# Attention units of 250 queries instead of 375, full PSUM banks, and two steps between changes of TensorE's tiling

## The chip, the cores and the metric

One core of a Trainium2 chip runs the whole program in one launch. The metric is the device time of that launch in microseconds (us). TensorE (PE in the profile) does the matrix products, VectorE (DVE) and ScalarE (ACT) read its results out of PSUM, GpSimd (POOL) works in SBUF and issues indirect DMAs, SyncE's queue (SPq) issues the direct ones.

## The reference

An audio tower of two layers over 8 streams (B = 8) of 750 tokens and 64 features: a convolutional tokenizer, then attention, a mixture of 8 experts, a phase-memory block and a second mixture, each with a residual. Only the attention of layer 0 is touched:

```python
q = jnp.einsum('btd,hrd->bhtr', x, Q)      # x: layer-normed h, (8, 750, 64); Q: (8, 32, 64)
k = jnp.einsum('bud,hrd->bhur', x, K)
scores = jnp.einsum('bhtr,bhur->bhtu', q, k) / sqrt(d)
attn = jax.nn.softmax(scores, axis=-1)
ctx = jnp.einsum('bhtu,bud->bhtd', attn, x)
out = jnp.einsum('bhtd,hde->bte', ctx, VO)  # VO: (8, 64, 64)
```

All of it is float32: 8 streams, 8 heads of 32 features, 750 queries against 750 keys.

## The kernel before, in words

**Units and steps.** The attention stage works in units of one stream, one pair of heads (`hp`, 4 of them) and one part of the queries (`th`). Before, a part is half of the queries (`HALF` = 375), so there are 8 x 4 x 2 = 64 units (`NQ`), and a unit has 6 steps, one for each tile of 125 keys (`c`): 384 steps. `place(m)` gives a unit's stream, pair and part.

**A step on TensorE** (the loop at the end of the stage, `for m ... for c ...`):

- `scores_t` (L627), one matmul for each of the two heads: transposed scores, 125 keys x 375 queries, with 32 contraction rows, into a PSUM bank of its own.
- the jobs of `maxima(m, c)`, two `score` jobs (L576): scores of the unit two ahead, untransposed, 125 queries x 375 keys, of which only the row maximum is wanted. They go to the ring (below). The unit two ahead is of the other pair of heads, so they lie on the two 32-row groups of the array that `scores_t` doesn't use.
- `shifts` (L638), bf16, 3 contraction rows: subtracts each query's maximum from the transposed scores by accumulation in the same bank.
- `values(x - 1)` (L654) of the step before: exp(scores) of 125 keys x 375 queries against the tokens, two heads as two column tiles of 64, accumulated over the six steps in the one bank `ctx_bank`.
- the other ring jobs due at this step (`ring_jobs`).

**The ring.** Three PSUM banks (0 to 2) are used in turn by all jobs that are not part of the step itself. Job k of the order list `order` takes bank k % 3, and TensorE waits on `ring_free` until job k - 3 has been read out. The jobs: `score` (read by VectorE's `reduce_max`, L1578), `shift` (a transposition of the maxima, L582), `proj` (queries and keys, L565, read by ScalarE, L1291), `out` (context times VO and the row sums, L616, read by VectorE: L1627, L1628, and after every second one L1632, L1633), `xt`, `logits` and `pos` (layer norm transposes and routing of the mixture, L590, L601, L608). Every engine walks through the same list in the same order, so VectorE reads the ring in the order in which TensorE fills it.

**From maxima to shift.** When the last `score` job of a unit has been reduced, VectorE joins the maxima (L1582), POOL splits them into three bf16 parts (five instructions, L1067 to L1071), TensorE transposes them (`shift`), VectorE copies them (L1588), and SyncE's queue writes them with two DMAs into `NS_` (L938), from where `shifts` reads them.

**Other banks.** Two pairs of banks (3 to 6, `st_bank`) hold the transposed scores of alternating steps; ScalarE's `exp_` reads one pair at a time (L1300) into one of four SBUF buffers. `ctx_out` (ScalarE, L1308) copies `ctx_bank` to SBUF after a unit's last step; `values` of the next unit waits for it.

**Around the stage.** Ahead of the loop, `before` holds 4 projections, and the maxima and shifts of units 0 and 1. Behind it, `after` holds the outputs and the routing of the last stream. `side_jobs` puts layer norms and routing of other engines at fixed steps.

The waits that matter:

```python
pe.wait_ge(ring_free[k % 3], k // 3)        # ring: wait for the job three before
pe.wait_ge(S["exp_done"], x - 1)            # scores_t of step x
pe.wait_ge(S["ctx_out"], m)                 # values, first step of unit m
```

Of the kernel before, what the change touches and what calls it, by code (L numbers as in the profile page):

```python
# [15 lines left out]
BF16 = mybir.dt.bfloat16  # L16
# [3 lines left out]
AX = mybir.AxisListType.X  # L20
# [4 lines left out]
HALF = L // 2  # L25
NB, KT = 9, 3
# [23 lines left out]
def build(nc, t, out):  # L50
    with ExitStack() as ctx:
# [89 lines left out]
        QH, at = view(0, [2, 2, L])  # L141
        KH, at = view(at, [2, 2, L])
        NS_, at = view(at, [2, HALF + 1], BF16)
        CT, at = view(at, [2, 4, L])
        PR, at = view(at, [4, 2, HALF], parts=R)
        MX, at = view(at, [2, 2, 6], parts=R)
        M1, at = view(at, [2, 6], parts=R)
        MR, at = view(at, [2, 6], parts=R)
        NM, at = view(at, [2, 18], BF16, parts=R)
        MT, at = view(at, [2, 126], BF16, parts=18)  # L150
# [154 lines left out]
        NU = 4 * B  # L305
# [49 lines left out]
        NQ = 8 * B  # L355

        def place(m):

            b, u = divmod(m, 8)
            return b, u // 2, u % 2  # L360

        def maxima(m, c):

            return [("score", m + 2, 2 * c + h2) for h2 in range(2)] if m + 2 < NQ else []

        def ring_jobs(m, c):

            b, hp, th = place(m)
            s = 12 * hp + 6 * th + c
            found = []  # L370
            if c == 1 and 2 <= m + 1 < NQ:
                found.append(("shift", m + 1))
            if b == 0 and s in (2, 3, 4, 5):
                found.append(("proj", 0, 1, (s - 2) // 2, s % 2))
            if b + 1 < B and s in (14, 16, 18, 20):
                found.append(("proj", b + 1, 0, (s - 14) // 4, (s - 14) // 2 % 2))
            if b + 1 < B and s in (26, 28, 30, 32):
                found.append(("proj", b + 1, 1, (s - 26) // 4, (s - 26) // 2 % 2))
            if b > 0 and 3 <= s < 27 and s % 2 == 1:
                found.append(("out", b - 1, (s - 3) // 4, (s - 3) // 2 % 2))  # L380
            if b < 2 and s in (24, 27):
                found.append(("xt", 1, b + 2, (s - 24) // 3))
            if b > 0:
                found += {35: [("xt", 2, b - 1, 0)], 36: [("xt", 2, b - 1, 1)], 38: [("logits", b - 1)],
                          42: [("pos", b - 1)]}.get(s, [])
            return found

        def side_jobs(m, c):

            b, hp, th = place(m)  # L390
            s = 12 * hp + 6 * th + c
            found = []
            if b < 2 and s in (4, 8, 15, 19):
                found.append(("ln_mean" if s in (4, 15) else "ln_std", 1, b + 2 + NP * (s >= 15)))
            if b > 0:
                if s in (28, 32):
                    found.append(("ln_mean" if s == 28 else "ln_std", 2, b - 1))
                if s == 39:
                    found += [("choose", b - 1), ("weigh", b - 1)]
                if s == 44:  # L400
                    found.append(("slots", b - 1))
                if s >= 45:
                    found += [("scatter", b - 1, 2 * (s - 45)), ("scatter", b - 1, 2 * (s - 45) + 1)]
# [9 lines left out]
        order = before + [x for m in range(NQ) for c in range(6)  # L413
                          for x in maxima(m, c) + ring_jobs(m, c) + side_jobs(m, c)] + after
# [63 lines left out]
        def _(pe):  # L478
# [74 lines left out]
            def ring(job):  # L553
# [5 lines left out]
                if kind == "proj":  # L559
                    _, b, g, qk, th = job  # L560
                    p, a = b % NP, b // NP
                    if ("xt", 1, b, 1) in ring_at:
                        ring_emptied(pe, ("xt", 1, b, 0))
                        ring_emptied(pe, ("xt", 1, b, 1))
                    last = pe.matmul(ps[:, 0:HALF], qkp[:, a, qk, g * 128:(g + 1) * 128],  # L565
                                     XT[:, p * L + th * HALF:p * L + (th + 1) * HALF], start=True, stop=True)
                elif kind == "score":
                    _, q, i = job
                    b, hp, th = place(q)
                    h2, half, j = i % 2, i // 2 % 2, 3 * th + i // 4  # L570
                    g, row = hp // 2, 64 * (hp % 2) + 32 * h2
                    if i == 0 and q % 4 == 0:
                        for qk in range(2):
                            for part in range(2):
                                ring_emptied(pe, ("proj", b, g, qk, part))
                    last = pe.matmul(ps[0:R, 0:HALF], QH[row:row + 32, b % 2, g, j * R:(j + 1) * R],  # L576
                                     KH[row:row + 32, b % 2, g, half * HALF:(half + 1) * HALF],
                                     start=True, stop=True, tile_position=(row, 0))
                elif kind == "shift":
                    q = job[1]  # L580
                    pe.wait_ge(S["shift_in"], q + 1)
                    last = pe.transpose(ps[0:18, 0:63].bitcast(BF16)[:, 0:R],  # L582
# [27 lines left out]
                else:  # L610
                    _, b, j, h = job
# [1309 lines left out]
```

## Time and profile before

| what | value |
|---|---|
| median of 3 runs | 1637.41 us (1635.68 to 1638.0) |
| the profiled execution | 1635.87 us |
| its span, first to last instruction | 1634.0 us |
| mean granted TensorE clock over the span | 0.854 of full |
| TensorE busy | 1303.5 us (80%) |
| VectorE busy | 986.9 us (60%) |
| ScalarE busy | 588.3 us (36%) |
| GpSimd busy | 443.3 us (27%) |

### The profile page before, as it was taken

Reading aid. Unit: us, or ns where it says so; the run is one execution under the profiler, and the core shown is the slowest. Engines: PE = TensorE matmul, PEld = TensorE weight load, DVE = VectorE, ACT = ScalarE, POOL = GpSimd, SP = SyncE. Lnnn points to the kernel's source line nnn. Section 1 sums busy time; section 2 is a strip of 40 time slices with the busy share of each in tenths; the row PEclk is TensorE's granted clock in tenths of the full one; section 3 lists DMA queues with packets and bytes.
Section 4 is the critical chain, followed back from the end, with each engine's and each line's share of the span. In section 5 each row is a group of like instructions: output and inputs, shape, how many; then the busy total and the mean of one; then the engine's idle time right before and its main releaser. Section 6 shows DMA issues by size and latency. Waiting matters only on the chain.

```text
span 1634.0 us, 21800 instructions
## 1 busy us (share of the span) xinstructions
PE 1303.5 (80%) x8045; PEld 668.8 (41%) x8045; DVE 986.9 (60%) x2165; ACT 588.3 (36%) x933; POOL 443.3 (27%) x797
## 2 busy tenths in 40 slices
PE   5589999999999999999999961750437658565895
PEld 4343344444444444444444331320216456454664
DVE  3355576666666666656667430212688988742798
ACT  1314444434444444444443310220144244322552
POOL 3112022302314013031130132007862362642000
PEclk9769999999999999999999855785667758656898
DMA  2100000000000000000000011121200000000000
GB/s 70 21 1 2 1 2 2 6 1 2 3 1 2 1 2 2 1 1 2 2 2 2 1 27 29 22 52 16 19 3 1 1 1 1 11 1 1 5 18 17
DMA packets 45974, 14.36 MB, mean 9 GB/s; under 512 B 43194, under 2 KB 44314, under 8 KB 45869
## 3 DMA queue, kind: packets, MB, share of 16 engines
q1 hardware_dynamic: 41261, 11.06, 3.1%
q0 software_dynamic: 4608, 1.91, 1.3%
q8 instruction: 65, 1.06, 0.3%
q14 instruction: 40, 0.33, 0.1%
HBM read 6.67 MB, written 7.17 MB: 8 GB/s over the span
## 4 chain that ended last, share of the span: by engine, by line
PE 64%; DVE 21%; POOL 5%; issue 4%; SPq 3%; DMA 2%; ACT 1%; POOLq 0%; DVEq 0%; ACTq 0%
PE psum L627 19%; PE psum L654 19%; PE psum L576 4%; PE psum L616 3%; PE psum L565 3%; PE psum L638 3%; DVE arena L1888 2%; DVE arena L1887 2%; PE psum L698 2%; DVE arena L1882 1%; SPq L952 1%; POOL lnst L1038 1%; SPq L926 1%; PE psum L710 1%; DVE lnst L1549 1%
## 5 line engine op out<-in xcount | busy, mean ns | idle before, releaser
L1578 DVE TENSOR_REDUCE arena<-psum 125x1 f32<-125x375 f32 x768 | 385.2, 543 | 227.3 <-PE psum L576 221.5
L1300 ACT ACTIVATE arena<-psum 125x750 f32<-125x750 f32 x384 | 305.9, 797 | 462.6 <-PE psum L638 456.8
L576 PE MATMUL psum<-arena 32*125 32x375 f32 x1536 | 385.2, 535 | 0.8 <-ACT arena L1291 0.7
L627 PE MATMUL psum<-arena 32*125 32x375 f32 x1536 | 352.7, 536 | 0.0
L654 PE MATMUL psum<-arena,XN 125*64 125x375 f32 x1536 | 333.9, 514 | 0.0
L627 PEld LDWEIGHTS psum<-arena 32*125 32x125 f32 x1536 | 115.6, 184 | 153.4 <-issue 130.7
L654 PEld LDWEIGHTS psum<-arena,XN 125*64 125x64 f32 x1536 | 77.1, 136 | 174.5 <-issue 173.8
L576 PEld LDWEIGHTS psum<-arena 32*125 32x125 f32 x1536 | 136.1, 184 | 23.7 <-DVE arena L1578 21.0
L638 PE MATMUL psum<-arena,onesb 3*125 3x375 bf16 x768 | 128.2, 327 | 0.0
L1067 POOL TENSOR_SCALAR arena<-arena 125x6 bf16<-125x6 f32 x64 | 15.9, 249 | 377.8 <-DVE arena L1582 377.4
L1142 POOL DMA_INDIRECT XN<-expert_out,slot_out x48 | 63.5, 1324 | 107.7 <-DMA expert_out<-arena 93.8
L540 PE MATMUL psum<-ident,XN 125*128 125x125 f32 x84 | 18.0, 379 | 91.9 <-POOL XN L1039 73.8
L784 PE MATMUL psum<-ident,arena 125*128 125x125 f32 x48 | 16.8, 361 | 70.2 <-DVE arena L1776 69.9
L616 PE MATMUL psum<-vox,arena 128*125 128x130 f32 x384 | 69.1, 307 | 3.8 <-DVE arena L1628 3.8
L1467 ACT ACTIVATE arena<-psum,wall 128x375 f32<-128x375 f32 x96 | 55.0, 574 | 45.2 <-PE psum L875 38.6
L638 PEld LDWEIGHTS psum<-arena,onesb 3*125 3x125 bf16 x768 | 54.0, 134 | 37.1 <-issue 3.1
L616 PEld LDWEIGHTS psum<-vox,arena 128*125 128x125 f32 x384 | 51.5, 195 | 40.5 <-issue 33.9
L1122 POOL DMA_INDIRECT expert_in<-XN,slot_in x48 | 58.8, 1226 | 23.2 <-issue 15.0
L565 PE MATMUL psum<-XT,qkp 128*128 128x375 f32 x128 | 59.2, 550 | 0.7 <-ACT XT L1277 0.7
L1038 POOL TENSOR_TENSOR lnst<-lnst,mhalf 125x12 f32<-125x12 f32 x14 | 32.2, 2298 | 99.8 <-DVE lnst L1558 99.8
L1269 ACT ACTIVATE arena<-XN 125x768 f32<-125x768 f32 x14 | 11.7, 839 | 124.4 <-DVE XN L1551 124.4
L1627 DVE RECIPROCAL arena<-psum 125x4 f32<-125x4 f32 x96 | 17.4, 182 | 59.2 <-PE psum L616 59.2
(322 smaller groups left out, 1989.6 us busy)
## 6 DMA issues: line engine op xcount, KB each, us to landing
arena<-arena SPq DMA_DIRECT2D x128, 2.2 KB
expert_in<-XN SPq DMA_DIRECT2D x8, 250.0 KB
arena<-expert_in SPq DMA_DIRECT2D x8, 250.0 KB
expert_out<-arena SPq DMA_DIRECT2D x8, 250.0 KB
out<-H SPq DMA_DIRECT2D x8, 187.5 KB
expert_in<-XN,slot_in POOLq DMA_INDIRECT x48
XN<-expert_out,slot_out POOLq DMA_INDIRECT x48, 3.9
arena<-in_L_ffn_w SPq DMA_DIRECT2D x2, 256.0 KB, 4.3
```

The source lines that it names most:

```text
L565: last = pe.matmul(ps[:, 0:HALF], qkp[:, a, qk, g * 128:(g + 1) * 128], XT[:, p * L + th * HALF:p * L + (th + 1) * HALF], start=True, stop ...
L576: last = pe.matmul(ps[0:R, 0:HALF], QH[row:row + 32, b % 2, g, j * R:(j + 1) * R], KH[row:row + 32, b % 2, g, half * HALF:(half + 1) * HAL ...
L616: last = pe.matmul(ps[0:R, i * 130:(i + 1) * 130], CT[:, b % 2, hp, j * R:(j + 1) * R], vox[:, hp, :], start=True, stop=True)
L627: pe.matmul(st_bank[x % 2][h2][0:R, 0:HALF], KH[row:row + 32, b % 2, g, c * R:(c + 1) * R], QH[row:row + 32, b % 2, g, th * HALF:(th + 1) ...
L638: last = pe.matmul(st_bank[x % 2][h2][0:R, 0:HALF], onesb[row:row + 3, 0:R], NS_[row:row + 3, th, 0:HALF], start=False, stop=True, tile_po ...
L654: last = pe.matmul(ctx_bank[64 * h2:64 * h2 + 64, 0:HALF], XN[:, p, c, a, :], PR[:, x % 4, h2, :], start=(c == 0), stop=(c == 5), tile_pos ...
L1038: link(pool.tensor_tensor(lnst[:, 3, p, :], lnst[:, 2, p, :], mhalf[0:R, 0:2 * NJ], ALU.pow))
L1122: pool.indirect_dma_start(out=xbuf, out_offset=bass.IndirectOffsetOnAxis(ap=slot_in[:, g:g + 1], axis=0), in_=XN[:, p, j, a, :], in_offset ...
L1142: pool.indirect_dma_start(out=XN[:, p, j, a, :], out_offset=None, in_=ybuf, in_offset=bass.IndirectOffsetOnAxis(ap=slot_out[:, g:g + 1], a ...
L1300: act.activation(PR[:, x % 4], psum[0:R, 3 + 2 * (x % 2):5 + 2 * (x % 2), 0:HALF], ACT.Exp)\
L1467: act.activation(dst, ps[:, 0:HALF], ACT.Relu, bias=b_).then_inc(done, 1)
L1578: dve.reduce_max(MX[:, q % 2, i // 2 % 2, col:col + 1], ps[0:R, 0:HALF], AX).then_inc(done, 1)
```

## The change

- A unit is one stream, one pair of heads and one third of the queries (`THIRD` = 250): 96 units, 3 steps each, 288 steps. A step takes two key tiles, so that a bank holds 2 x 250 = 500 columns.
- In a step the `shifts` come first (one matmul of 500 columns for each head, `start=True`), then `scores_t` of the first key tile, then `score` jobs, then `scores_t` of the second key tile, and then a second pair of `score` jobs where there is one.
- A unit has 6 `score` jobs of 500 columns instead of 12 of 375: a query tile against keys 0 to 499 (two tiles, two heads), and both query tiles against keys 500 to 749 in one bank. `max_step` sets their steps; two jobs fall on a step, but four on each of the first six steps, and the last nine have none.
- TensorE takes the steps in pairs: everything of steps k and k + 1 up to the scores, then `values(k - 2)`, the ring jobs due at k, `values(k - 1)`, and the ring jobs due at k + 1. ScalarE's order: `exp_(k)`, a `ctx_out` if one is due, `exp_(k + 1)`, a `ctx_out` if one is due, then projections.
- Projections are split by half of the streams (`a`): 64 contraction rows each, two jobs in a row on the two 64-row groups of the array. Queries and keys of all 8 streams are kept, so all projections are made in the first three streams. The outputs are split likewise: `out_pair` issues both jobs of a query tile together, 8 matmuls of 65 columns, alternating between two row groups and two ring banks.
- `before` holds 8 projections (4 pairs), and the maxima and shift of unit 0 only.

```diff
-        NQ = 8 * B
+        NQ = 12 * B
...
+        def max_step(k):
+
+            return (k - 3) // 2 if k < 15 else k - 9
+
+        max_at = {}
+        for k in range(3, 3 * NQ):
+            max_at.setdefault(max_step(k), []).append((k // 3, k % 3))
+        shift_at = {min(max_step(3 * q + 2) + 2, 3 * q - 1 - q % 2): q for q in range(1, NQ)}
+
+        def maxima(x):
+
+            return [("score", q, 2 * tile + h2) for q, tile in max_at.get(x, []) for h2 in range(2)]
...
+        proj_at = {(0, 1 + i): job for i, job in enumerate(projections(0, 1))}
+        for p in range(1, NP):
+            for i, job in enumerate(projections(p, 0) + projections(p, 1)):
+                proj_at[(p - 1, 6 + 2 * i)] = job
+
+        def ring_jobs(x):
+
+            b, s = divmod(x, 36)
             found = []
+            if x in shift_at:
+                found.append(("shift", shift_at[x]))
+            if (b, s) in proj_at:
+                found += [proj_at[(b, s)] + (a,) for a in range(2)]
+            if b > 0 and 3 <= s < 15 and s % 2 == 1:
+                found += [("out", b - 1, (s - 3) // 2, h) for h in range(2)]
+            if b < 2 and s in (31, 33):
+                found.append(("xt", 1, b + 2, (s - 31) // 2))
             if b > 0:
+                found += {21: [("xt", 2, b - 1, 0)], 22: [("xt", 2, b - 1, 1)], 24: [("logits", b - 1)],
+                          27: [("pos", b - 1)]}.get(s, [])
             return found
...
-        before = [("proj", 0, 0, qk, th) for qk in range(2) for th in range(2)]
-        for q in range(2):
-            before += [("score", q, i) for i in range(12)] + [("shift", q)]
+        before = [job + (a,) for job in projections(0, 0) for a in range(2)]
+        before += [("score", 0, i) for i in range(6)] + [("shift", 0)]
...
+        order = before + [job for x in range(0, 3 * NQ, 2) for job in
+                          maxima(x) + maxima(x + 1) + ring_jobs(x) + side_jobs(x) + ring_jobs(x + 1) + side_jobs(x + 1)] + after
...
+            def out_pair(b, j):
+
+                for h in range(2):
+                    k = ring_at[("out", b, j, h)]
+                    if k >= 3:
+                        pe.wait_ge(ring_free[k % 3], k // 3)
+                if j == 0:
+                    pe.wait_ge(S["ctx_out"], 12 * (b + 1))
+                for hp in range(4):
+                    for h in range(2):
+                        r = slice(64 * h, 64 * h + 64)
+                        ps = ring_bank[ring_at[("out", b, j, h)] % 3]
+                        last = pe.matmul(ps[0:R, hp * (D + 1):(hp + 1) * (D + 1)], CT[r, b % 2, hp, j * R:(j + 1) * R],
+                                         vox[r, hp, h * (D + 1):(h + 1) * (D + 1)], start=True, stop=True,
+                                         tile_position=(64 * h, 0))
+                        if hp == 3:
+                            last.then_inc(S["ring_full"], 1)
...
+                if h2 == 0:
+                    if x >= 2:
+                        pe.wait_ge(S["exp_done"], x - 1)
+                    if cc == 0:
+                        pe.wait_ge((S["shift_dma0"], S["shift_dma1"])[m % 2], 32 * (m // 2 + 1))
+                pe.matmul(st_bank[x % 2][h2][0:R, 0:2 * THIRD].rearrange("r (i c) -> r i c", i=2), onesb[row:row + 3, 0:R],
+                          NS_[row:row + 3, th, :].unsqueeze(1).to_broadcast([3, 2, THIRD]),
                           start=True, stop=False, tile_position=(row, 0))
...
+            ring_in(before)
+            for k in range(0, 3 * NQ, 2):
+                for x in (k, k + 1):
+                    mx = maxima(x)
                     for h2 in range(2):
+                        shifts(x, h2)
                     for h2 in range(2):
+                        scores_t(x, 0, h2)
+                    ring_in(mx[0:2])
+                    for h2 in range(2):
+                        scores_t(x, 1, h2)
+                    ring_in(mx[2:])
+                if k:
+                    values(k - 2)
+                    ring_in(ring_jobs(k))
+                    values(k - 1)
+                ring_in(ring_jobs(k + 1) if k else ring_jobs(k) + ring_jobs(k + 1))
+            values(3 * NQ - 2)
+            values(3 * NQ - 1)
...
-            for m in range(NQ):
-                for c in range(6):
-                    exp_(m, c)
-                    if c == 0 and m:
-                        ctx_out(m - 1)
...
+            for x in range(0, 3 * NQ, 2):
+                exp_(x)
+                if x >= 2 and (x - 2) % 3 == 2:
+                    ctx_out((x - 2) // 3)
+                exp_(x + 1)
+                if x >= 2 and (x - 1) % 3 == 2:
+                    ctx_out((x - 1) // 3)
...
+                    h2, tile = i % 2, i // 2
+                    if tile < 2:
+                        dve.reduce_max(MX[:, q % 2, 0, 2 * h2 + tile:2 * h2 + tile + 1], ps[0:R, 0:2 * THIRD], AX)\
+                           .then_inc(done, 1)
+                    else:
+                        dve.reduce_max(MX[:, q % 2, 1, 2 * h2:2 * h2 + 2],
+                                       ps[0:R, 0:2 * THIRD].rearrange("r (n c) -> r n c", n=2), AX).then_inc(done, 1)
```

The rest of the diff fits sizes (`MX`, `M1`, `NM`, `MT`, `NS_`, `QH`, `KH`, `PR`), counts of semaphores and the steps of the side jobs to the new units. The three ring banks, the two pairs of score banks, the four buffers of `exp_` and the one `ctx_bank` stay.

## Rows read from the trace of the kernel before

**Rows 1.** Stretches: busy us (instructions) of PE, PEld, DVE, ACT, POOL; clock; DMA.

```profile
104.00:110.80 6.80, 6.80 (x35) 3.01 (x34) 2.31 (x5) 1.59 (x2) 0.00 (x0) 0.50 0.01 3
110.80:926.60 815.80, 815.66 (x5888) 333.86 (x5882) 527.28 (x1222) 357.14 (x501) 182.45 (x516) 1.00 0.01 2
926.60:958.50 31.90, 31.90 (x99) 10.43 (x98) 2.07 (x11) 7.79 (x11) 12.62 (x24) 0.50 0.02 1
```

**Rows 2.** Timeline of TensorE, one step with a shift ahead and a projection behind.

```profile
809.88 0.22 PE L582 MATMUL psum<-identb,arena 125*18 125x125 bf16 x1
810.03 0.58 PE L627 MATMUL psum<-arena 32*125 32x375 f32 x2
810.04 0.66 PE L576 MATMUL psum<-arena 32*125 32x375 f32 x2
810.45 0.48 PE L627 MATMUL psum<-arena 32*125 32x375 f32 x2
...
810.76 0.33 PE L638 MATMUL psum<-arena,onesb 3*125 3x375 bf16 x2
811.02 0.85 PE L654 MATMUL psum<-arena,XN 125*64 125x375 f32 x4
811.80 0.90 PE L565 MATMUL psum<-XT,qkp 128*128 128x375 f32 x2
812.63 0.58 PE L627 MATMUL psum<-arena 32*125 32x375 f32 x2
```

**Rows 3.** Timeline of all engines, step 1 right behind step 0, half clock.

```profile
105.41 0.82 PE L576 MATMUL psum<-arena 32*125 32x375 f32 x1
...
105.67 1.00 DVE L1578 TENSOR_REDUCE arena<-psum 125x1 f32<-125x375 f32 x2 [1.36 <-PE psum L576]
105.71 0.83 PE L627 MATMUL psum<-arena 32*125 32x375 f32 x2
...
106.27 0.28 PEld L576 LDWEIGHTS psum<-arena 32*125 32x125 f32 x1 [0.23 <-DVE arena L1578]
```

**Rows 4.** Groups of instructions by form in the stage: VectorE's maximum.

```profile
L1578 DVE TENSOR_REDUCE arena<-psum 125x1 f32<-125x375 f32 x744 | 372.8, 543 | 206.2 <-PE psum L576 200.4 <-issue 3.8
```

**Rows 5.** Timeline of all engines where a unit ends: its last values, then ScalarE's copy.

```profile
406.86 0.85 PE L654 MATMUL psum<-arena,XN 125*64 125x375 f32 x4
...
407.75 0.48 ACT L1308 ACTIVATE arena<-psum 128x375 f32<-128x375 f32 x1
```

**Rows 6.** Timeline of TensorE around one output job.

```profile
210.60 0.71 PE L616 MATMUL psum<-vox,arena 128*125 128x130 f32 x4
211.24 0.58 PE L627 MATMUL psum<-arena 32*125 32x375 f32 x2
```

**Rows 7.** Timeline of VectorE behind a second output job.

```profile
215.74 0.17 DVE L1627 RECIPROCAL arena<-psum 125x4 f32<-125x4 f32 x1
215.94 0.42 DVE L1628 TENSOR_TENSOR arena<-psum,arena 125x256 f32<-125x256 f32 x1
...
217.49 0.23 DVE L1633 TENSOR_TENSOR H<-H,arena 125x64 f32<-125x64 f32 x1
```

**Rows 8.** Chain of waits ahead of the loop (start, us, what).

```profile
74.67 5.35 PE psum L565 x8
...
80.54 0.14 issue
...
91.69 9.55 PE psum L576 x24
...
101.26 0.56 DVE arena L1578
...
104.06 0.92 PE psum L627 x2
```

**Rows 9.** Timeline of TensorE, one step of the last twelve, at half clock.

```profile
929.81 1.61 PE L627 MATMUL psum<-arena 32*125 32x375 f32 x4
...
933.11 1.61 PE L627 MATMUL psum<-arena 32*125 32x375 f32 x4
```

More of the change, by code:

```diff
@@ L353, in build @@
         ln_at = {x: k for k, x in enumerate(lns)}
-        NQ = 8 * B
+        NQ = 12 * B
         def place(m):
[L359 to L369, printed above, removed]
-            found = []
[L371 to L382, printed above, removed]
+            b, u = divmod(m, 12)
+            return b, u // 3, u % 3
@@ L569, in ring @@
                     b, hp, th = place(q)
-                    h2, half, j = i % 2, i // 2 % 2, 3 * th + i // 4
+                    h2, tile = i % 2, i // 2
                     g, row = hp // 2, 64 * (hp % 2) + 32 * h2
-                    if i == 0 and q % 4 == 0:
+                    if i == 0 and q % 6 == 0:
                         for qk in range(2):
                             for part in range(2):
[L575 to L578, printed above, removed]
+                                ring_emptied(pe, ("proj", b % NP, g, qk, part, b // NP))
+                    parts = [(tile, 0, 2 * THIRD, 0)] if tile < 2 else [(n, 2 * THIRD, L, n * THIRD) for n in range(2)]
+                    for n, lo, hi, at_ in parts:
+                        j = 2 * th + n
+                        last = pe.matmul(ps[0:R, at_:at_ + hi - lo], QH[row:row + 32, b, g, j * R:(j + 1) * R],
+                                         KH[row:row + 32, b, g, lo:hi], start=True, stop=True, tile_position=(row, 0))
                 elif kind == "shift":
@@ L609, in ring @@
                     last = pe.matmul(ps[0:R, 0:NJ * E0], ones[0:R, 0:R], SO[:, 0:NJ, :], start=False, stop=True)
-                else:
-                    _, b, j, h = job
-                    for i in range(2):
-                        hp = 2 * h + i
-                        if j == 0 and i == 0:
-                            pe.wait_ge(S["ctx_out"], 8 * b + 4 * h + 4)
-                        last = pe.matmul(ps[0:R, i * 130:(i + 1) * 130], CT[:, b % 2, hp, j * R:(j + 1) * R],
-                                         vox[:, hp, :], start=True, stop=True)
@@ L665, in _, with ring_in @@
+                last.then_inc(S["pv_done"], 1)
+            def ring_in(jobs_):
+                for job in jobs_:
+                    if job[0] == "out":
+                        if job[3] == 0:
+                            out_pair(job[1], job[2])
+                    else:
+                        ring(job)
+            ring_in(before)
+            for k in range(0, 3 * NQ, 2):
+                for x in (k, k + 1):
+                    mx = maxima(x)
                     for h2 in range(2):
-                        scores_t(m, c, h2)
@@ new lines, in _ @@
+                    ring_in(mx[0:2])
+                    for h2 in range(2):
+                        scores_t(x, 1, h2)
[7 more added lines that the diff above has]
+            values(3 * NQ - 1)
+            ring_in([job for job in after if job in ring_at])
@@ L1058, in _ @@
                 kind = job[0]
[L1059 removed]
+                if kind == "score" and job[2] == 5:
                     q = job[1]
```

163 lines of the change are left out of this document (69 added, 94 removed).

## The prediction

> **What bounds the kernel now.** I read the busy time by stretch first. From 110.8 to 926.6 us TensorE is busy for all but 0.14 of 815.8 us at the full clock, VectorE for 65% and ScalarE for 44% [rows 1]. So the attention stage, 104.0 to 958.5 us (854.5 us), is TensorE's, and only what shortens its sequence counts. The slices of the page say nothing of gaps inside it, so I went to the timeline of one step [rows 2]. The second passes of `scores_t` begin 0.42 us after the first (810.03, 810.45), `shifts` 0.31 later: a pass of 375 columns takes 0.31, and 0.11 is the first weight load, uncovered. `shifts` (0.16, one pass) is followed 0.26 later by `values`, so 0.10 passes before the column tiling starts; `values` lasts 0.78, two passes of 0.31 and 0.15 of load and change. A step is 0.99 + 0.78 = 1.77 us, 0.36 of it load and change. The maxima (L576) start 0.01 behind `scores_t` and run beside it: free for TensorE as long as their bank is.
>
> The chain of waits says what that freedom costs when row tiles follow without `values` between. At steps 0 and 1 the third of four maxima starts at 105.41, ahead of its step's scores at 105.71; the fourth's weights load at 106.27, released by VectorE's reduction of the first, begun at 105.67 [rows 3]. The ring has three banks; the fourth job waits 0.60 us from the start of that reduction.
>
> The Trainium skill (TensorE: Matmul & The Clock Gate, "Part 3: Packing small matmuls") says that matmuls start and end strictly in program order. Rows 3 don't agree: a later job's pass started 0.30 us before an earlier one's. The consequence of such order is a rival below.
>
> **Part 1, fewer changes of tiling.** Same columns as before, in pairs of steps. Row part of a pair: load 0.05, then for each step a shift of 500 columns (0.21) and two key tiles of 250 (4 passes of 0.21, 0.83), and the change, 0.09: 2.25 us with nothing waited for. 
>
> **Part 2, the ring inside a pair.** Each pair has four maxima in one row part and three banks. First: load 0.11, two passes of 500 columns 0.83. Then the lag to VectorE: the third starts on the first's rows when that ends, 105.41, and the reduction starts 0.26 later [rows 3], at half clock; I take 0.21 at full clock, bounds 0.13 (all of it in the slower clock) and 0.26 (none). The reduction is 0.54 for 375 columns [rows 4]; for 500 at most 0.72 in proportion, at least 0.61 (the spacing of a back-to-back pair, 0.46, in proportion); I take 0.68, nearest to proportion less a fixed part. Release 0.06. The fourth maxima can load at 1.88 us, streams 0.94 (load and passes), and the change follows: `values` starts at 2.92 instead of 2.25. The pair is 4.76 us, **+0.67**, on 137 pairs **+92 us** (0.6 to 0.75: 82 to 103). The second key tile of that step is queued behind this wait, but ends at 2.4, covered. The values, 1.84, hide the other three reductions. The maxima were hidden entirely before.
>
> **Part 3, `ctx_bank`.** Where k is 4 modulo 6, `values(k - 2)` ends a unit and `values(k - 1)` begins the next, and between them ScalarE must copy the one bank. Before, a row part lay between. Old case: the copy starts 0.89 after the values' load and takes 0.48 [rows 5]. New: 1.10 (0.21 more passes), copy 0.38 (125 columns fewer), 0.14 back to TensorE [rows 8], load 0.05: streaming resumes at 1.67 instead of 0.89. **+0.78 x 48 = +37 us** (0.6 to 1.0: 29 to 48). `exp_(k + 1)` is behind this copy in ScalarE's queue; it ends some 5.4 us into the pair, and is wanted at 6.6, so nobody waits.
>
> **Part 4, outputs.** An old output job adds 0.64 to a step [rows 6], 0.11 a pass. `out_pair` does 8 passes on each row group side by side, 0.88 + 0.2 = 1.1 for two jobs. But both land ahead of a row part. VectorE needs 0.62 for a reciprocal and a product, the same for the second, and then 1.36 for the sum and the addition (215.74 to 217.72 [rows 7] is 1.98 for the second job with them). It starts 0.12 into the row part, frees the second maxima's bank at 0.8, the third's at 1.4, and takes up the first maximum at 2.75; the fourth's load is at 3.5, not 1.88: +1.6. Per pair 2.7, **42 pairs: 113 us**. Before: the stage less 680 of steps, 50 of projections (60 x 0.83, 811.80 to 812.63 [rows 2]), 9 of shifts (62 x 0.15, 809.88 to 810.03 [rows 2]), 14 of half-clock tail and 3 of cold start leaves 99; 32 small jobs (`xt`, `logits`, `pos`), 166 passes at up to 0.16, are 22 to 27 of it. I take 22, so 84 outputs cost 77. Change **+36 us** (between +10, if the sum and addition don't hold the maxima, and +45).
>
> **Part 5, projections, shifts, small jobs.** 28 pairs in the loop: 18 split two values (0.98 each), 3 elsewhere (2.7 together), 7 fall in the gaps of part 3 (0.2): 22 us against 50, **-28**. 48 of 96 shifts lie in those gaps too, 7 against 9: **-2**. Small jobs 20 against 22: **-2**. VectorE, POOL, and the queue of SyncE have one or two pairs, over 4.8 us each, between a unit's last maxima and its shift, and as much again to the first use; the chain from the last reduction to TensorE is 2.8 us (101.26 to 104.06 [rows 8]), so the 192 DMAs stay hidden.
>
> **Part 6, start and tail.** Ahead of the loop, 12.4 us per unit of maxima (91.69 to 104.06 [rows 8]) are paid twice. Now: projections 7.2 (eight jobs by pairs through three banks, against 5.4 and 0.5), six maxima of 500 columns at half clock 6.7, chain 2.8, and the DMA of the first shift, which nothing hides, some 3.3: the loop starts at 94.6 instead of 104.0, **-9**. The first three pairs carry eight maxima each, the first of them on the same row groups as the scores, from a cold start: 10.8, 12 and 7.9 us with 3.4 around them, against 12.3: **+22**, and the old cold start of 3 goes (**-3**). The old tail without maxima ran 31.9 us at half clock [rows 1], 3.3 a step [rows 9], from the twelve small matmuls of the routing on; now the routing of stream 6 falls where maxima still run, so I expect the tail at full clock, **-14** (0 if not).
>
> **Sum.** -91 + 92 + 37 + 36 - 28 - 2 - 2 - 9 + 22 - 3 - 14 = +38. The rest, 651 us before and after, is unchanged. The profiled execution took 1635.9 (span 1634.0 and 1.9 around it), 1.5 below the median; so 1674, and **1676 us** on the scale of the median.
>
> **Rivals.**
> 1. *The forecast*: the changes of tiling saved are given back to the ring and `ctx_bank`. For it: rows 3, the same situation. Chance 0.69, 1645 to 1705.
> 2. *The ring doesn't hold the pair*, and it comes out faster. Place: the fourth maxima. If the first bank were free before the scores end (wait under 0.39 instead of 0.67), the sum turns negative; with no wait there and none behind outputs, 1676 - 92 - 67 = 1517. It would need a reduction of 500 columns in 0.4; rows 3 and 4 speak against. Chance 0.13 with everything between, 1517 to 1634, most of it near the top through smaller outputs and start.
> 3. *The clock falls* in pairs with outputs, where TensorE idles over 1 us and small matmuls stand. The old tail, of half as many active rows, fell to 0.50 [rows 1], and a step there costs 3.3 instead of 1.77. If half of 42 such pairs ran at half clock, +4.5 each, +95: 1770. Chance 0.10.
> 4. *Matmuls in order after all*: the first maxima wait for the scores ahead of them, 0.45 per pair, 137 pairs: +62, 1738. Against: rows 3. Chance 0.04.
> 5. *A wash*, within 0.2% (3.3 us, what this measurement can tell from no change): 0.04.
>
> **Numbers.** The range takes the forecast's own and the near side of the clock's: 1643 to 1722. Faster 0.13, same 0.04, slower 0.83.
>
> **What would show it.** Right: a distance of some 4.8 us between first shifts of plain pairs; weight loads of L576's counterpart released by VectorE, some 1.9 us into each pair; a gap of 0.7 us on TensorE between values released by ScalarE's copy, 48 times; VectorE's maximum near 0.68 us; an attention stage of about 902 us instead of 854.5. Wrong: plain pairs of 4.1 us; maxima released by nobody; the clock at 0.50 inside the stage; a tail still at half clock.

## The result and the profile after

| what | before | after |
|---|---|---|
| median | 1637.7 us (4 runs, 1635.68 to 1640.59) | 1691.84 us (4 runs, 1690.93 to 1701.6) |
| ratio | | 1.0343 (95%: 1.0302 to 1.0384) |
| the profiled execution, its span | 1635.87, 1634.0 | 1690.93, 1689.2 |
| mean granted clock | 0.854 | 0.848 |
| loop starts | 103.99 | 92.24 |
| attention stage | 854.5 us | 918.0 us (92.24 to 1010.2) |

Slower by 3.4%, against 1676 forecast. The span grew by 55.2 us: the stage by 63.5, what follows it by 3.5, and the loop starts 11.8 earlier.

Busy time by stretch, of the kernel after, with the columns of [rows 1]:

```profile
92.20:121.20 29.00, 28.52 (x105) 17.18 (x105) 10.65 (x19) 5.79 (x8) 2.13 (x10) 0.50 0.00 1
121.20:1010.20 889.00, 836.56 (x7644) 504.74 (x7642) 512.91 (x1110) 338.16 (x438) 224.58 (x695) 0.98 0.01 2
```

TensorE was busy for all but 0.14 us of the long stretch before [rows 1]. Now it is idle for 52 of 889, and the clock is below full in places. The two largest idle times of its matmuls in the stage, as the page's groups of the kernel after give them (busy, mean ns, then idle before and what ended it), beside VectorE's maximum, which answers to [rows 4], and ScalarE's copy:

```profile
L591 PE MATMUL psum<-arena 32*125 32x500 f32 (+1 forms) x1536 | 463.6, 525 | 32.8 <-DVE arena L1617 23.7
L1617 DVE TENSOR_REDUCE arena<-psum 125x1 f32<-125x500 f32 x384 | 242.9, 673 | 145.7 <-PE psum L591 144.7
L682 PE MATMUL psum<-arena,XN 125*64 125x250 f32 x2304 | 299.5, 391 | 14.4 <-ACT arena L1344 14.4
L591 PEld LDWEIGHTS psum<-arena 32*125 32x125 f32 x1536 | 203.6, 188 | 111.8 <-DVE arena L1617 62.2
L1344 ACT ACTIVATE arena<-psum 128x250 f32<-128x250 f32 x96 | 36.5, 380 | 155.5 <-PE psum L682 155.5
```

Both waits that the prediction named are there: maxima (L591) wait for VectorE's reductions, `values` (L682) for the copy of `ctx_bank`. The 14.4 us over 48 gaps are 0.30 each; a gap costs more (0.79, below), because the last passes before it and small jobs within it count as busy.

Three kinds of pairs are told apart below. A plain pair has its four maxima and no other ring job; a gap pair has the copy of `ctx_bank` between its two `values`; a tail pair, at the end of the stage, has no maxima. The timeline of a plain pair after, all engines, is where [rows 2] and [rows 3] have their answer (start, length; in brackets the idle time before and what ended it):

```profile
191.60 0.42 PE L654 MATMUL psum<-arena,onesb 3*125 3x500 bf16 x2
...
192.76 1.26 DVE L1620 TENSOR_REDUCE arena<-psum 125x2 f32<-125x500 f32 x2 [0.84 <-PE psum L591]
...
193.50 0.18 PEld L591 LDWEIGHTS psum<-arena 32*125 32x125 f32 x1 [0.52 <-DVE arena L1620]
...
194.02 0.58 PE L591 MATMUL psum<-arena 32*125 32x500 f32 x1
...
194.53 1.91 PE L682 MATMUL psum<-arena,XN 125*64 125x250 f32 x16
...
196.37 0.42 PE L654 MATMUL psum<-arena,onesb 3*125 3x500 bf16 x2
```

The first reduction starts 1.16 into the pair, the fourth maxima's weights load at 1.90 (193.50), `values` start at 2.93 and the pair ends at 4.77. The prediction had 1.88, 2.92 and 4.76. Next pair, TensorE:

```profile
196.39 0.69 PE L591 MATMUL psum<-arena 32*125 32x500 f32 x2
196.63 0.58 PE L663 MATMUL psum<-arena 32*125 32x250 f32 x4
...
199.29 1.07 PE L682 MATMUL psum<-arena,XN 125*64 125x250 f32 x8
200.29 0.22 PE L596 MATMUL psum<-identb,arena 125*12 125x125 bf16 x1
200.93 1.07 PE L682 MATMUL psum<-arena,XN 125*64 125x250 f32 x8 [0.42 <-ACT arena L1344]
201.93 0.42 PE L654 MATMUL psum<-arena,onesb 3*125 3x500 bf16 x2
```

and the copy between them, in ScalarE's timeline:

```profile
200.41 0.38 ACT L1344 ACTIVATE arena<-psum 128x250 f32<-128x250 f32 x1 [1.71 <-PE psum L682]
```

The copy starts 1.12 behind the start of the unit's last values (rows 5 had 0.89 at 375 columns; 1.10 was predicted), and the next unit's values start at 1.64 (1.67 predicted). The first two lines of the same fence bear on the order of matmuls: the maxima come behind `scores_t` in the program and start 0.24 ahead.

An output pair, VectorE and TensorE, answers to [rows 6, 7]. First VectorE:

```profile
735.49 0.18 DVE L1670 RECIPROCAL arena<-psum 125x4 f32<-125x4 f32 x1 [0.80 <-PE psum L638]
735.71 0.43 DVE L1671 TENSOR_TENSOR arena<-psum,arena 125x256 f32<-125x256 f32 x1
...
736.72 1.03 DVE L1675 TENSOR_REDUCE arena<-arena 125x64 f32<-125x512 f32 x1
737.78 0.23 DVE L1676 TENSOR_TENSOR H<-H,arena 125x64 f32<-125x64 f32 x1
737.93 1.26 DVE L1620 TENSOR_REDUCE arena<-psum 125x2 f32<-125x500 f32 x2
```

The second job's product ends at 736.69; the sum over heads and the addition run to 738.01, and the first maximum of a pair that began at 735.38 comes only behind them, at 737.93 (the records overlap by 0.08). TensorE meanwhile:

```profile
735.39 0.42 PE L654 MATMUL psum<-arena,onesb 3*125 3x500 bf16 x2
...
738.65 0.68 PE L591 MATMUL psum<-arena 32*125 32x500 f32 x1 [0.82 <-DVE arena L1620]
...
739.68 1.91 PE L682 MATMUL psum<-arena,XN 125*64 125x250 f32 x16
```

The distance between first shifts of pairs, over the loop, at full clock:

| pair | predicted | measured |
|---|---|---|
| plain | 4.76 | 4.767 |
| no maxima (tail) | 4.09 | 4.10 |
| gap for `ctx_bank` (with shift) | +0.78 | 5.556, +0.79 |
| outputs, cost per output pair | +2.7 | +2.40 (six pairs and the one behind take 49.6 instead of 35.2) |
| a pair of projections, in a pair right behind a gap pair | +0.98 | +0.98 |
| the same in a gap pair | +0.2 | +0.34 |
| the same in a pair right ahead of a gap pair | +0.98 | +1.73 |
| first three pairs together | 34.1 | 39.8 |

### The profile page after: what moved, and what is told of

It is laid out like the page before. It is cut to its first block, busy times and chain, and to the rows that moved or that the text cites. A ratio compares the mean times of both kernels' runs of the same rounds, so it can differ in the third digit from the quotient of the medians.

```text
span 1689.2 us, 25593 instructions
## 1 busy us (share of the span) xinstructions
PE 1308.7 (77%) x9805; PEld 844.2 (50%) x9805; DVE 972.5 (58%) x2037; ACT 567.6 (34%) x869; POOL 476.5 (28%) x957
## 4 chain that ended last, share of the span: by engine, by line
PE 57%; DVE 27%; POOL 5%; issue 4%; SPq 3%; DMA 2%; ACT 2%; POOLq 0%; DVEq 0%; ACTq 0%
PE psum L682 17%; PE psum L591 14%; PE psum L663 6%; PE psum L638 3%; DVE arena L1675 3%; PE psum L654 2%; DVE arena L1931 2%; DVE arena L1671 2%; PE psum L576 2%; DVE arena L1930 2%; PE psum L735 2%; DVE arena L1925 1%; SPq L989 1%; DVE arena L1617 1%; ACT arena L1344 1%
## 5 line engine op out<-in xcount | busy, mean ns | idle before, releaser
L591 PE MATMUL psum<-arena 32*125 32x500 f32 (+1 forms) x1536 | 463.6, 525 | 32.8 <-DVE arena L1617 23.7
L1336 ACT ACTIVATE arena<-psum 125x1000 f32<-125x1000 f32 x288 | 288.8, 1003 | 407.2 <-PE psum L663 407.1
L663 PE MATMUL psum<-arena 32*125 32x250 f32 x2304 | 347.0, 392 | 0.0
L1617 DVE TENSOR_REDUCE arena<-psum 125x1 f32<-125x500 f32 x384 | 242.9, 673 | 145.7 <-PE psum L591 144.7
L682 PE MATMUL psum<-arena,XN 125*64 125x250 f32 x2304 | 299.5, 391 | 14.4 <-ACT arena L1344 14.4
L591 PEld LDWEIGHTS psum<-arena 32*125 32x125 f32 x1536 | 203.6, 188 | 111.8 <-DVE arena L1617 62.2
L682 PEld LDWEIGHTS psum<-arena,XN 125*64 125x64 f32 x2304 | 152.4, 139 | 170.2 <-issue 80.7
L663 PEld LDWEIGHTS psum<-arena 32*125 32x125 f32 x2304 | 208.9, 186 | 10.9 <-issue 2.3
L1620 DVE TENSOR_REDUCE arena<-psum 125x2 f32<-125x500 f32 x192 | 125.1, 674 | 34.8 <-PE psum L591 33.7
L654 PE MATMUL psum<-arena,onesb 3*125 3x500 bf16 x576 | 120.9, 403 | 4.1 <-DMA arena<-arena 4.1
L638 PE MATMUL psum<-vox,arena 64*125 64x65 f32 x768 | 57.0, 291 | 9.7 <-ACT arena L1328 4.6
```

Of the source, the lines that this page charges most:

```text
L591: last = pe.matmul(ps[0:R, at_:at_ + hi - lo], QH[row:row + 32, b, g, j * R:(j + 1) * R], KH[row:row + 32, b, g, lo:hi], start=True, stop= ...
L638: last = pe.matmul(ps[0:R, hp * (D + 1):(hp + 1) * (D + 1)], CT[r, b % 2, hp, j * R:(j + 1) * R], vox[r, hp, h * (D + 1):(h + 1) * (D + 1) ...
L654: pe.matmul(st_bank[x % 2][h2][0:R, 0:2 * THIRD].rearrange("r (i c) -> r i c", i=2), onesb[row:row + 3, 0:R], NS_[row:row + 3, th, :].unsq ...
L663: last = pe.matmul(st_bank[x % 2][h2][0:R, i * THIRD:(i + 1) * THIRD], KH[row:row + 32, b, g, c * R:(c + 1) * R], QH[row:row + 32, b, g, t ...
L682: last = pe.matmul(ctx_bank[64 * h2:64 * h2 + 64, 0:THIRD], XN[:, p, c, a, :], PR[:, x % 4, h2, i * THIRD:(i + 1) * THIRD], start=(c == 0) ...
L1336: act.activation(PR[:, x % 4], psum[0:R, 3 + 2 * (x % 2):5 + 2 * (x % 2), 0:2 * THIRD], ACT.Exp)\
```

## The experiments

Theory A is the forecast's: in a pair the fourth maxima waits for the ring's first bank, the second `values` for the copy, and behind outputs everything waits for VectorE. Theory B, in several forms, puts the loss elsewhere: in TensorE's own passes, in the smaller units, in the small matmuls of the outputs, or in one common cause.

| kernel | median us | ratio to before (95%) | a stream, us | plain pair, us |
|---|---|---|---|---|
| before | 1637.7 | 1 | 106.3 | 3.54 (2 old steps) |
| after | 1691.84 | 1.0343 (1.0302 to 1.0384) | 108.7 | 4.767 |
| half_max | 1647.29 | 1.0037 (1.0016 to 1.0058) | 104.0 | 4.506 |
| single | 1591.87 | 0.9687 (0.9651 to 0.9723) | 96.2 | 4.39 (2 steps) |
| defer_sum | 1639.94 | 1.0002 (0.9982 to 1.0022) | 100.7 | 4.766 |
| ctx_twice | 1721.28 | 1.0501 (1.0463 to 1.0539) | 111.1 | 4.767 |
| pair_old | 1710.2 | 1.0432 (1.0401 to 1.0464) | 119.1 | 3.80 (2 old steps) |
| single_defer | 1571.58 | 0.9590 (0.9564 to 0.9616) | 94.4 | 4.39 |
| single_half | 1569.5 | 0.9574 (0.9545 to 0.9602) | 94.1 | 4.39 |
| single_ctx_twice | 1585.37 | 0.9678 (0.9646 to 0.9709) | 96.2 | 4.39 |
| pair_half_defer | 1594.65 | 0.9741 (0.9707 to 0.9775) | 96.2 | 4.505 |

Each ratio is to runs of the kernel before that were taken beside that kernel's, so it can differ a little from the quotient of the two medians. "A stream" is the seventh of eight, first shift to first shift. It ran at full clock except in `pair_old`, where 3.4 us of it are at half clock; its fourth stream, all at full clock and with the same jobs, takes 117.6. A step before makes 750 columns of scores (375 for each of two heads) against 1000 after, so 48 old steps and 36 new ones make the same scores. But in the kernel before and in `pair_old` the seventh stream also holds eight projections, 6.6 us at 0.83 each, and in the others none, since they have made all of theirs by the third stream. For the same content the 106.3 of the kernel before are to be read as 99.7.

**half_max.** The reductions read every second column, those of both forms; the diff shows one.

```diff
-    dve.reduce_max(MX[...], ps[0:R, 0:2 * THIRD], AX)
+    dve.reduce_max(MX[...], ps[0:R, 0:2 * THIRD:2], AX)
```

> The changed kernel with every maximum taken over every second column of its bank (250 elements instead of 500), so it leaves out half of the maxima's work; the softmax is the same for any shift. Theory A (the fourth maxima of a pair wait for VectorE's reduction of the first): a reduction takes about 0.41 us instead of 0.67, a plain pair 4.50 instead of 4.77, 137 pairs give 36 us, the cold start some 5 more: about 1650 us. Theory B (TensorE itself, passes and changes of tiling, sets the pair, the reductions lie beside it): no change, 1692 us.

Measured: 1647.29. A reduction takes 0.415 instead of 0.673, which is 0.26 less, and the plain pair is 0.26 shorter, the gap pair too (5.295), and the tail pair is unchanged at 4.10. VectorE's reduction stands on TensorE's path to its full length.

**single.** The pairing alone is undone: TensorE, ScalarE and the order list go step by step.

```diff
-for k in range(0, 3 * NQ, 2):
-    for x in (k, k + 1):
-        ...
-    values(k - 2); ring_in(ring_jobs(k)); values(k - 1)
+for x in range(3 * NQ):
+    ...
+    values(x - 1)
+    ring_in(ring_jobs(x))
```

> The changed kernel with the pairing alone undone: same units of 250 queries, same 500-column banks, same halves of projections and outputs, but values of step x - 1 behind the scores of step x, step by step. Theory A (ring wait and the gap at ctx_bank come from the pairing): a plain step takes 1.18 + 1.01 = 2.2 us, two of them 4.4 instead of 4.77, no gap of 0.78 at unit ends, clock stays at full: about 1590 us, faster than the kernel before. Theory B (the longer stage comes from smaller units and more passes, and pairing saves what it was meant to save): two changes of tiling more per pair, +0.36 x 144 = +52 us: about 1744 us.

Measured: 1591.87, below both kernels. The page's group of the maxima in this kernel, to be set against the 32.8 us above:

```profile
L590 PE MATMUL psum<-arena 32*125 32x500 f32 (+1 forms) x1536 | 392.1, 520 | 0.4 <-ACT arena L1323 0.4
L1609 DVE TENSOR_REDUCE arena<-psum 125x1 f32<-125x500 f32 x384 | 242.9, 674 | 141.7 <-PE psum L590 140.4
```

The reductions last as long as in the kernel after, and no matmul waits for them: between two row parts `values` give VectorE the time. From 128 to 908 us TensorE is idle for 1.46 us, at full clock:

```profile
128.00:908.00 780.00, 778.54 (x7610) 468.92 (x7606) 515.21 (x1110) 340.96 (x436) 222.94 (x694) 1.00 0.01 2
```

A step is 2.195, two are 4.39. The paired tail, where nothing is waited for, has 4.10. So one change of tiling fewer is worth **0.29 us a pair**, 42 us over 144 pairs, and 288 x 2.195 = 632 against the old 680 says that the rest of the change in a step is worth 48: full banks, with smaller units and the shifts in first place, which no run parted.

**defer_sum.** VectorE keeps the sum over heads and the addition until a job comes that is no maximum.

```diff
+    if job[0] != "score" and job[0] != "proj":
+        settle()                       # reduce_sum, addition of the outputs owed
...
-    link(dve.reduce_sum(OR, ...)); dve.tensor_tensor(H[...], ...)
+    owed.append(job)
```

> The changed kernel with VectorE's sum over heads and addition to H (L1675 and the line behind it, 1.3 us) of every output pair moved behind the four maxima that follow in its order. Theory A (behind outputs, the fourth maxima wait because VectorE takes up the first one 1.3 us late): 42 output pairs lose up to 1.3 us each, -55 us, and if the short falls of the clock go with the idle time up to 15 more: 1625 to 1640 us. Theory B (output pairs are long through their own 16 small matmuls): no change, 1692 us.

Measured: 1639.94, no difference from before. VectorE's timeline, the same pair of the program as above:

```profile
703.33 0.42 DVE L1685 TENSOR_TENSOR arena<-psum,arena 125x256 f32<-125x256 f32 x1
703.67 1.41 DVE L1634 TENSOR_REDUCE arena<-psum 125x2 f32<-125x500 f32 x2
```

The maxima follow the product at once, and that pair goes from 6.138 to 4.81. Of six output pairs five become 1.33 shorter, and so does the plain pair behind: 8.0 a stream, 56 over seven streams; the median fell by 51.9.

**ctx_twice.** ScalarE copies `ctx_bank` twice.

```diff
     act.activation(CT[...], ctx_bank[:, 0:THIRD], ACT.Copy)
+       .then_inc(S["ctx_twice"], 1)
+    act.wait_ge(S["ctx_twice"], m + 1)
+    act.activation(CT[...], ctx_bank[:, 0:THIRD], ACT.Copy)
```

> The changed kernel with ScalarE's copy of ctx_bank made twice, the second behind the first, before values may go on. Theory A (48 of the 96 copies stand between values and values of one pair and TensorE waits for them): 0.38 + 0.1 us more in 48 gaps, +21 to +24 us: about 1714 us, and plain pairs unchanged at 4.77. Theory B (the copy is hidden by the shift and other jobs between): no change, 1692 us.

Measured: 1721.28, 29 more. ScalarE in a gap, and `values` behind it:

```profile
664.97 0.38 ACT L1344 ACTIVATE arena<-psum 128x250 f32<-128x250 f32 x1 [1.71 <-PE psum L682]
665.38 0.38 ACT L1347 ACTIVATE arena<-psum 128x250 f32<-128x250 f32 x1
```

```profile
665.90 1.07 PE L682 MATMUL psum<-arena,XN 125*64 125x250 f32 x8 [0.36 <-ACT arena L1347]
```

The gap pair is 5.967, +0.41, and the plain pair stays at 4.767. 48 x 0.41 is 20. In the profiled execution, 27.4 longer, most of the rest is a stretch at half clock, 17.1 us from 937 on, which the kernel after has not: its last stream, first shift to last, takes 109.0 instead of 101.0, of which the copies are some 2.

**single_ctx_twice.** The same edit in `single`.

> The changed kernel without the pairing, with ScalarE's copy of ctx_bank made twice. Theory A (without pairing a row part of 1.2 us lies between the last values of a unit and the first of the next, and the copy, 0.38 and a second 0.38 with 0.1 between, lies beside it, with ScalarE's exponential of 1.0 us ahead of nothing that waits): no gap, or the tail of one, 0 to 8 us over 95 unit ends: 1590 to 1600 us. Theory B (TensorE waits for the copy at every unit end, pairs or not): 95 x 0.41 = +39 us, about 1630.

Measured: 1585.37, against 1591.87 for `single`: no cost. A stream takes 96.2 in both; the 6 us between them are the start, which is at half clock for 27.3 us here and for 37.5 there.

```profile
550.49 0.38 ACT L1339 ACTIVATE arena<-psum 128x250 f32<-128x250 f32 x1
550.90 0.38 ACT L1342 ACTIVATE arena<-psum 128x250 f32<-128x250 f32 x1
```

```profile
553.23 1.07 PE L681 MATMUL psum<-arena,XN 125*64 125x250 f32 x8
```

Both copies are done by 551.28, and `values` start at 553.23, behind a row part. The copy is paid only where the pairing puts two `values` side by side.

**pair_old.** The pairing alone, put into the kernel before: steps of 375 columns and one key tile, two at a time.

```diff
-for m in range(NQ):
-    for c in range(6):
+for k in range(0, 6 * NQ, 2):
+    for x in (k, k + 1):
         ...                       # scores_t, maxima, shifts of step x
-        values(x - 1); ring_jobs
+    values(k - 2); ring_jobs(k); values(k - 1); ring_jobs(k + 1)
```

> The kernel before (units of 375 queries, 375-column banks, 6 steps a unit, unsplit projections and outputs) with the pairing of steps alone put in: scores, maxima and shifts of two steps, then values of the two steps before. Unit ends fall between pairs, so no gap at ctx_bank. Theory A (four maxima of a pair share three banks, the fourth waits): a plain pair 3.78 us instead of 2 x 1.77, +44 us over the stage; behind every second output job VectorE takes up the first maximum late, +26; projections between two values +9: 1700 to 1720 us, slower than the kernel before. Theory B (pairing saves one change in and out of the column tiling per pair, 0.25 to 0.36 us): 1570 to 1600 us, faster.

Measured: 1710.2. One pair with outputs on both sides, TensorE:

```profile
497.84 0.57 PE L581 MATMUL psum<-arena 32*125 32x375 f32 x1
497.93 0.80 PE L632 MATMUL psum<-arena 32*125 32x375 f32 x4
498.25 0.47 PE L581 MATMUL psum<-arena 32*125 32x375 f32 x1
499.63 0.57 PE L581 MATMUL psum<-arena 32*125 32x375 f32 x1 [0.90 <-DVE arena L1589]
```

and in the page's groups:

```profile
L581 PE MATMUL psum<-arena 32*125 32x375 f32 x1536 | 478.5, 532 | 39.0 <-DVE arena L1589 38.3
```

The plain pair is 3.80 where two old steps took 3.54, and its tail pair without maxima 3.19: the pairing gives 0.35 and the ring takes 0.61. No gap for `ctx_bank` is left here, since six steps of a unit are three whole pairs. At full clock a stream is 11.3 us longer (117.6 against 106.3): 6.2 in 24 pairs of +0.26, some 3.3 more in pairs behind output jobs, as in the pair shown, whose fourth maxima load 2.6 us in, and 1.3 more in pairs that hold projections alone. The harm is the pairing's, not the full banks'.

**single_half.** The maxima over every second column, in `single`.

> The changed kernel without the pairing, with every maximum over every second column of its bank (half of the maxima's work left out). Theory A (without pairing a plain step waits for no reduction): plain steps stay at 2.2 us; only steps behind outputs and the start gain, 8 to 14 us in all: 1578 to 1584 us. Theory B (the ring holds TensorE there too, 0.26 us per two steps as with pairs): about 1556 us.

Measured: 1569.5. Plain steps are unchanged, 2.195, so the reduction is hidden in them, as A said. But the gain over `single` is 22 us where A had 8 to 14: output steps with a shift go from 3.64 to 3.39, a stream from 96.2 to 94.1, and the first from 120.2 to 115.4, in which the start is at half clock for 10 us less. The reduction still counts behind outputs; that and the start's clock I had sized too small.

**single_defer.** The sum over heads deferred as in `defer_sum`, in `single`.

> The changed kernel without the pairing, and with VectorE's sum over heads and addition moved behind the maxima that follow. Theory A (behind an output pair the next step's second maxima wait for the reduction of the first, 0.5 us, because of that sum): 42 x 0.5 = 21 us less than without the move, about 1571 us, the fastest so far; the wait of the second maxima for the bank of the first output stays. Theory B (outputs cost their own matmuls only): no change against 1592 us.

Measured: 1571.58, as expected, with the whole computation done: 4.1% under the kernel before and 7.1% under the kernel after. The deferral is worth 1.8 us a stream here and 8.0 in the paired kernel: the chain of the outputs costs less where two maxima wait behind it than where four do. (6 us of the 20 under `single` are the start again, 27.3 us at half clock instead of 37.5.)

**pair_half_defer.** Both remedies in the paired kernel.

> The changed kernel, pairing kept, with both remedies: maxima over every second column (half of their work left out) and the sum over heads moved behind the maxima. Theory A (two separate causes, the reduction's length in every pair and the sum behind outputs): the gains add but for the part that half_max had behind outputs, 1640 - 137 x 0.26 = 1604, with the first steps 1600: still above the 1592 of the kernel without pairing and with whole maxima, since the gap at ctx_bank and 0.4 us of the ring's wait stay. Theory B (one cause, VectorE's load as a whole, which either remedy cures): no better than the better of the two, about 1640.

Measured: 1594.65. The gains were 44.6 and 51.9 alone and 97.2 together, so they are two causes and not one seen twice; A's 1604 was 9 too high, since it let part of the first gain go behind the outputs. The paired kernel with half of the maxima's reading left out is still 23 us slower than `single_defer` with all of it.

## Why the prediction was right, and where its sizes were off

**The sign and the mechanism held.** Fewer changes of tiling are paid back to the ring and to `ctx_bank`. `single` against the kernel after is that statement by itself. In the seventh stream, 108.7 against 96.2, 18 pairs at 0.377 (4.767 less 4.39) are 6.8 us, six gaps of 0.79 are 4.7, the outputs are 1.9 more, and shifts that fall into the gaps give back 0.9: 12.5. Seven such streams (the first and the last count as one together) are 88, the clock below is some 14, and the loop starts 4 earlier (92.24 against 96.34): 98, as measured in the profiled executions (1689.2 less 1591.4).

**Parts 1 and 2** came out to 0.01 us a pair: 4.10 and 4.767 against 4.09 and 4.76. But the text credited its -91 to "fewer changes of tiling". The runs split it: 48 of it come from the fuller steps, 42 from the pairing, and the +92 of part 2 belong to the pairing alone. An edit that the prediction took as one is two, one good and one bad. Two of its workings are to be set right, though neither moved the forecast. The terms named for the row part add to 2.22, not 2.25; the measured tail pair, 4.10, bears out the 2.25.
**Part 3** held: +0.79 against +0.78, in the tail too (4.89 against 4.10).

**Part 4, outputs, was too dear**: 2.40 a pair, not 2.7, 12.6 us less over 42. The matmuls cost 1.02, not 1.1: the first output pair of a stream, which waits for nothing, takes 5.786. The wait costs 1.37, not 1.6: the plain pair behind the outputs takes 6.138. In it the weights of the fourth maxima load at 738.65, 3.27 us in, where I had 3.5, because VectorE's chain was shorter: its first maximum starts 2.55 into the pair, not 2.75.

**Part 5, projections, was too cheap.** Pairs come in threes: in the first the second `values` end a unit, in the second no unit ends, and the third is the gap pair. With projections in both of the first two, the second takes 1.73 more than a plain one, not 0.98. ScalarE's timeline has the reason: at the end of the first pair it copies `ctx_bank` and only then that pair's projections, and the maxima of the second pair, which reuse their banks, wait for it:

```profile
156.32 0.38 ACT L1344 ACTIVATE arena<-psum 128x250 f32<-128x250 f32 x1 [1.77 <-PE psum L682]
156.59 0.85 ACT L1328 ACTIVATE arena<-psum 128x375 f32<-128x375 f32 x2
```

```profile
157.12 0.55 PEld L591 LDWEIGHTS psum<-arena 32*125 32x125 f32 x4 [0.32 <-ACT arena L1328]
```

I named the queue behind `ctx_out` for `exp_` and not for the projections. Where outputs follow such projections they wait for the same copies (TensorE is idle for 1.17 us ahead of the outputs at 373.56), and that pair takes 2.22 more than without projections, four times. The 24 pairs behind the first three lose 28.5 us to projections; 22 had been set for all 28. With small jobs this is about 8 us.

**Part 6.** The loop starts at 92.24 (94.6 predicted, 2.4 better). The first three pairs take 14.0, 16.1 and 9.7, 39.8 in all, where I had 10.8, 12 and 7.9 and 3.4 around them, 34.1. The chain of waits of the kernel after, start and length, shows the first pair's scores and maxima one after the other at half clock; I had counted part of them side by side:

```profile
92.91 0.83 PE psum L663 x4
93.75 1.67 PE psum L591 x4
95.41 0.83 PE psum L663 x4
96.25 1.96 PE psum L591 x4
```

The tail ran at full clock, as forecast: the clock falls at 1015.5, behind the stage.

**Rival 3, the clock, came true in small.** Granted clock by stretch, after:

```profile
244.00:247.50 3.50, 2.33 (x35) 2.13 (x36) 1.31 (x5) 1.10 (x3) 0.83 (x2) 1.00 0.02 6
247.50:257.70 10.20, 10.20 (x52) 5.03 (x45) 3.92 (x8) 2.87 (x4) 1.07 (x5) 0.50 0.00 0
257.70:271.40 13.70, 11.15 (x107) 6.62 (x105) 9.84 (x23) 4.03 (x6) 4.14 (x10) 1.00 0.01 3
271.40:285.10 13.70, 12.58 (x71) 7.18 (x69) 5.52 (x13) 3.14 (x5) 1.53 (x4) 0.50 0.00 1
```

Ahead of each of the two falls TensorE stands idle, for 1.17 of 3.5 us and for 2.55 of 13.7. There are four falls in the stage, 37.5 us at half clock (10.2, 13.7, 10.2, 3.4), all of them less than 5 us behind an output job, and they cost about 14 us beside the same pairs at full clock. The forecast priced the event at 95 or nothing, and missed the case between.

**The sum.** The stage was 16 us longer than the 902 predicted: clock +14, first pairs +5.7, projections and small jobs +8, plain pairs +1, outputs -12.6. The earlier loop (-2.4) and the part behind the stage (+3.5) nearly cancel. That the 16 us between 1676 and 1691.8 are about what the clock took is luck: the other errors happened to cancel.

**Still open.** Why the clock falls where it does. Every kernel with pairing has such falls between 200 and 960 us (six in `pair_old`, five each in `defer_sum` and `ctx_twice`, four in `half_max`, three in `pair_half_defer`). The four unpaired kernels have none inside their stages, and the kernel before has one only in its tail, from 926.6 on [rows 1]. The unpaired kernels have the same small matmuls, so these alone do not do it. What differs is TensorE's idle time: from 200 to 860 us it is 57 us in `ctx_twice`, 43 in the kernel after, 35 in `half_max`, 31 in `pair_old`, 19 in `defer_sum` and in `pair_half_defer`, and at most 2.4 in the unpaired kernels and the kernel before. All but one fall begin within about 5 us of an output job. The exception, in `pair_old`, begins at 789.5, 34 us behind the last output but inside the twelve small matmuls of a routing job (788.16 to 789.57). So idle time near small matmuls is what goes with the falls, but its amount does not set them: `defer_sum` has less than half of the idle time and still 30.7 us at half clock in five falls, against 37.5 in four. A fourth ring bank, which would keep the pairing without its first wait, wasn't tried either: all eight banks are in use.

## What to carry to other kernels

Before moving work together to save changes of an engine's mode, count for each buffer pool how many of its jobs now fall between two points where the consumer can catch up: with three banks, the fourth job in a row pays one whole reduction and the lag before it starts, here 0.67 us to save 0.29. The same holds for a single accumulator: two accumulations back to back expose its copy. Of two edits made together, run each alone: here everything but the pairing gave some 3%, and the change as a whole lost 3.4%.

## What the runs showed of the hardware that I had not expected

- TensorE's clock can fall to half inside a stage in which it is busy for 94% of the time (836.56 of 889 us), for 3.4 to 13.7 us at a time (17.1 in `ctx_twice`), and it returns with the same program going on.
- A reduction that reads every second column of PSUM takes 0.415 us for 250 of 500 columns against 0.673 for all: 0.258 for 250 columns, so some 0.16 of each is fixed, if both forms pay the same for a column. The 0.543 for 375 columns in the kernel before [rows 4] lies on the same line (0.16 and 375 times 0.00103).
- A float32 pass of 250 columns takes 0.21 us, as long as the bf16 pass of 500 columns (`shifts`), and nothing shows on top of it: sixteen passes of `values` take 1.84 us (194.53 to 196.37), which is two at a time on the two column tiles, 8 x 0.21 and 0.16 for the weights and the change.
